# Involution stage: the running maximum is taken chunk by chunk from PSUM, and ScalarE copies the weights of GpSimd's taps

## The chip, the cores and the metric

The kernel runs on one core of one Trainium2 chip. The metric is the device time of one execution in microseconds. Five engines run side by side and meet at semaphores: TensorE (PE), VectorE (DVE), ScalarE (ACT), GpSimd (POOL) and SyncE (SP, which only issues DMAs here).

## The reference, cut to what matters

The program is an involution layer followed by attention and a token-routed feed-forward layer. Only the involution is touched. Per pixel it computes 49 weights (a 7x7 window) for each of 32 channel groups, takes a softmax over the 49, and sums 49 shifted copies of the projected image with them:

```
sub2 = x1[:, :, None] - unfold_patches(x2)
y = relu(bn_eval(feat, ...))            # 34 channels x 49 taps x pixels
y = conv1x1(y, cw1)
y = relu(bn_eval(y, ...))
wgt = softmax(conv1x1(y, cw2, cb2), axis=2)     # over the 49 taps
for i in range(K):
    for j in range(K):
        out = out + patch(i, j) * wgt[:, :, idx][:, :, None]
```

The softmax subtracts the maximum over the taps, and its denominator is summed beside the products (as a ninth plane) and divided out at the end.

## The kernel before

The 56x56 image is cut into 14 blocks of 4 rows; 128 partitions hold 4 images x 32 groups. `conv_stage` works on two blocks at once in a slot: for the next block `a` it makes the logits (the chain), for the current block `b` it forms and sums the 49 products. There are 15 slots: the first has only `a`, the last only `b`, and 13 have both. `slots` writes them out for each engine, the middle ones inside a loop. Every engine runs its own list in program order.

In a slot the steps u = 0 to 19 are "pairs": DVE multiplies the weights of two taps with the window (`pair`, 39 taps) into one of two `prod` buffers; the last 10 taps are GpSimd's `own` products. PE adds every tap's nine planes to the accumulators in PSUM banks 4 to 7 through an identity matrix (`add`). ACT copies the weights of a pair twice: to PSUM banks 2 and 3 for DVE (`weights`) and into the ninth plane of `prod` for PE (`denominators`).

The chain of block `a` goes through 14 chunks c (half a kernel row each), one for each step u = c + 1 (`CH_AT`). A chunk passes PE `first` (two matmul groups), ACT `second` (ReLU from PSUM), PE `second`, ACT `third` (adds the bias and writes the logits `lg`). All chunks of a slot with both blocks use the same two PSUM banks, so PE's `first` of a chunk waits until ACT's `third` of the chunk before has emptied them. GpSimd's `z` and ACT's `first(i)` (a ReLU) prepare the input of each kernel row i. DVE takes the maximum of the logits row by row (`rowmax`, 6 instructions) and folds the 7 columns of a row (`fold`, 3 instructions) into `mx`; GpSimd subtracts it (`shift`), ACT exponentiates (`expo`). For block `a`, GpSimd does `shift` 0 and 1 at the end of the slot, behind `own(8)`; ACT follows with `expo` 0 and 1 and `weights` 0, after which the next slot's first pair can start.

GpSimd's `own` has two buffers, so `own(k)` waits until PE has added `own(k-2)` (`own_used`), which PE does at step u = 8 + k, behind that step's pair.

```
OWN_AT = [NPAIR_D - OWN + k for k in range(OWN)]      # 10 .. 19
POOL_ORDER = [..., ("own", 0), ("own", 1), ("z", 6)] + [("own", k) for k in range(2, OWN - 1)]
```

Of the kernel before, what the change touches and what calls it, by code (L numbers as in the profile page):

```python
# [339 lines left out]
NMAX = K7 + 1  # L340


class Blk:
# [24 lines left out]
def conv_stage(nc, planes, x2_dram, a1_dram, pf_dram, cw1_bd, cw2_bd, ident_dram, conv_dram, keep):  # L368
    ctx = ExitStack()
    with ctx:  # L370
# [73 lines left out]
        @block.gpsimd  # L444
        def _(pool):
            def z(a, i):
                q = a.q(i)
                if i == 0:
                    pool.wait_ge(x_in[a.par], 32 * (a.half + 1))
                if not (a.early(1) and i < 2):  # L450
                    pool.wait_ge(mm1, 2 * (q - 1))
                o = y1[a.qpar(i)][:].rearrange("p j (h w) -> p j h w", w=W)
                x1 = a1[a.par][:].rearrange("p (h w) -> p h w", w=W).unsqueeze(1).broadcast_to([P, K7, RW, W])
                row = x2w[a.par][:, i:i + RW, 0:W]
                x2 = bass.AP(row.tensor, row.offset, [row.ap[0], [1, K7], row.ap[1], row.ap[2]])
                pool.tensor_tensor(o, x1, x2, ALU.subtract).then_inc(z_ready, 1)  # L456

            def shift(b, i):
                pool.wait_ge(maxed, b.n + 1)
                if not b.early(1):  # L460
                    pool.wait_ge(den_in, NPAIR_D * (b.n - 1) + FREE_ROW_PAIRS if i < FREE_ROW else NPAIR_D * b.n)
                if i == FREE_ROW and not b.early(1):
                    pool.wait_ge(own_ready, 2 * OWN * b.n)
# [80 lines left out]
        def _(act):  # L544
# [18 lines left out]
            def denominators(b, p):  # L563
# [2 lines left out]
                    act.wait_ge(summed, NPAIR_D * b.n + p - 1)  # L566
                act.activation(prod[p % 2][:, 0:n, :, SHARE], tap_pair(p), ACT.Copy).then_inc(den_in, 1)

            def slot(a, b):
                def first(i):  # L570
                    act.wait_ge(z_ready, a.q(i) + 1)
# [14 lines left out]
                def third(c):  # L586
                    act.wait_ge(mm2, a.g(c) + 1)
                    i, h, k = c // 2, c % 2 * 2, chain_bank(b, c)
                    if b and c % 2 == 0:
                        act.wait_ge(shifted, b.q(i) + 1)  # L590
                    act.activation(lg[:, i, h:h + 2].rearrange("p h j w -> p h (j w)"), ps[:, k:k + 2, 0:CW],  # L591
                                   ACT.Identity, bias=par[:, CB2:CB2 + 1]).then_inc(logit, 1)

                if b is None:
                    first(0)
                    for c in range(NCH):
                        second(c)
                        if c >= 1:
                            third(c - 1)
                        if c % 2 == 0 and c + 2 < NCH:  # L600
                            first(c // 2 + 1)
                    third(NCH - 1)
# [30 lines left out]
        def _(v):  # L633
# [9 lines left out]
                                den.unsqueeze(2).broadcast_to([P, B, SHARE, W]), ALU.mult).then_inc(divided, 1)  # L643

            def slot(a, b):
                def rowmax(i):
                    if i == 0:
                        return
                    v.wait_ge(logit, a.g(2 * i + 2))
                    if i == 1 and b and not b.early(1):  # L650
                        v.wait_ge(divided, 2 * b.n)
                    if i > 1:
                        v.wait_ge(ranmax, NMAX * a.n + i - 1)
                    v.tensor_tensor(run[:], lg[:, i], lg[:, 0] if i == 1 else run[:], ALU.max).then_inc(ranmax, 1)

                def fold():
                    v.wait_ge(ranmax, NMAX * a.n + K7 - 1)
                    v.tensor_tensor(run[:, :, 0:3], run[:, :, 0:3], run[:, :, 4:7], ALU.max).then_inc(ranmax, 1)
                    v.wait_ge(ranmax, NMAX * a.n + K7)
                    v.tensor_tensor(run[:, :, 0:2], run[:, :, 0:2], run[:, :, 2:4], ALU.max).then_inc(ranmax, 1)  # L660
                    v.wait_ge(ranmax, NMAX * a.n + K7 + 1)
                    if b:
                        v.wait_ge(shifted, K7 * a.n)
                    v.tensor_tensor(mx[:].rearrange("p (h w) -> p h w", w=W), run[:, :, 0], run[:, :, 1], ALU.max).then_inc(maxed, 1)  # L664

                def pair(p):
                    n = min(2, ND - 2 * p)
# [27 lines left out]
        def _(pe):  # L695
# [5 lines left out]
            def slot(a, b):  # L701
                def first(c):
                    i, hh = c // 2, c % 2
                    if hh == 0:
                        pe.wait_ge(relu1, a.q(i) + 1)
                        pe.wait_ge(pf_in[a.qpar(i)], 16 * B * a.qhalf(i))
                    k = chain_bank(b, c)
                    if b is None:
                        if c >= 2:
                            await_ge(logit, a.g(c) - 1)  # L710
# [33 lines left out]

                def pair(p, k):
                    if k == 0:
                        pe.wait_ge(den_in, NPAIR_D * b.n + p + 1)
                        await_ge(prod_ready, NPAIR_D * b.n + p + 1)
                    mm = add(prod[p % 2][:, k], p == 0 and k == 0, False)
                    if 2 * p + k == min(2 * p + 1, ND - 1):  # L750
                        mm.then_inc(summed, 1)

                def own(k):
                    await_ge(own_ready, 2 * (OWN * b.n + k + 1))
                    mm = add(own_buf[k % 2], False, k == OWN - 1)
                    if k < OWN - 1:
                        mm.then_inc(own_used, 1)
# [1726 lines left out]
```

## Time and profile before

| what | value |
|---|---|
| time, median of 3 executions | 3697.45 us (3691.7 to 3697.88) |
| profiled execution, span from first to last instruction | 3768.7 us (no other time of this execution is on record) |
| PE busy | 3044.6 us (81%) |
| DVE busy | 2563.3 us (68%) |
| ACT busy | 2010.5 us (53%) |
| POOL busy | 2040.6 us (54%) |
| mean granted TensorE clock | 0.919 |

The span is 71.25 us longer than the median of the timed executions. The involution's slots lie between about 235 us and 1714 us of it; the shares above mix them with the rest. In the timeline rows quoted below, a number in square brackets is the engine's idle time just before, with what ended it.

### The profile page before, as it was taken

The numbers are of one execution on the slowest core, as the hardware profiler recorded it, in microseconds if no ns is written. First come the engines' busy times: TensorE is split into PE (matmuls) and PEld (weight loads), VectorE is DVE, ScalarE is ACT, GpSimd is POOL, SyncE is SP. The second block draws the span as 40 slices with busy tenths as digits, with TensorE's granted clock in tenths as the row PEclk, the third lists the DMA queues.
The fourth block names the chain that finished last, engine by engine and source line by source line (L and its number), as shares of the span: only waits on it lengthen the run. The fifth ranks groups of instructions, "written<-read, shape, count | busy, mean of one in ns | idle before, by whom it ended". The sixth has DMA issues, their size and how long they took to land. (4 is left out here: it accounts for less than half of the span.)

```text
span 3768.7 us, 102003 instructions
## 1 busy us (share of the span) xinstructions
PE 3044.6 (81%) x42638; PEld 1539.3 (41%) x42638; DVE 2563.3 (68%) x2229; ACT 2010.5 (53%) x3451; POOL 2040.6 (54%) x1112
## 2 busy tenths in 40 slices
PE   4767788877777788764999899989999987586797
PEld 1224444433443444432433434343435343364565
DVE  6359999999999999996745755574667456443212
ACT  1175566666555566632676666657566754333120
POOL 1169888889898888874622434060416123332422
PEclk9889999999899999896999999999999998797898
DMA  5621111211111112103111111210221112343344
GB/s 195 194 76 47 58 37 58 61 58 59 52 56 50 57 35 61 51 12 97 27 27 64 41 27 37 74 29 19 61 69 28 27 45 98 115 132 113 123 134 127
DMA packets 169418, 257.31 MB, mean 68 GB/s; under 512 B 81584, under 2 KB 128600, under 8 KB 165912
## 3 DMA queue, kind: packets, MB, share of 16 engines
q1 hardware_dynamic: 157120, 219.82, 19.2%
q0 software_dynamic: 11360, 30.95, 2.6%
q8 instruction: 357, 5.85, 0.6%
q14 instruction: 77, 0.63, 0.1%
q10 hardware_dynamic: 504, 0.05, 0.0%
HBM read 152.23 MB, written 79.27 MB: 61 GB/s over the span
## 5 line engine op out<-in xcount | busy, mean ns | idle before, releaser
L741 PE MATMUL ps<-prod,ident 32*32 32x504 f32 x17472 | 936.4, 646 | 259.4 <-issue 182.7
L678 DVE TENSOR_TENSOR prod<-ps,win 128x3584 f32<-128x3584 f32 x280 | 1054.6, 3789 | 97.6 <-PE ps L741 50.9
L1405 POOL TENSOR_TENSOR pool<-kv 128x768 f32<-128x768 f32 (+1 forms) x200 | 349.8, 1756 | 541.5 <-ACT kv L1539 494.4
L741 PEld LDWEIGHTS ps<-prod,ident 32*32 32x32 f32 x17472 | 382.7, 108 | 464.1 <-issue 412.5
L1583 ACT ACTIVATE phq<-ps 128x896 f32<-128x896 f32 x448 | 391.3, 919 | 80.4 <-PE ps L1915 76.8
L456 POOL TENSOR_TENSOR y<-a1w,x2w 128x1568 f32<-128x1568 f32 x98 | 346.0, 3538 | 132.0 <-PE ps L722 114.9
L465 POOL TENSOR_TENSOR ex<-lg,mx 128x1568 f32<-128x1568 f32 x98 | 345.1, 3541 | 16.1 <-DVE mx L664 15.9
L1915 PE MATMUL ps<-qst,sel 96*128 96x448 bf16 x1120 | 297.2, 362 | 17.0 <-ACT sx L1568 8.4
L560 ACT ACTIVATE ps<-ex 128x448 f32<-128x448 f32 x280 | 148.4, 533 | 296.6 <-DVE prod L678 296.6
L1690 DVE TENSOR_TENSOR pool<-ps,kv 128x1280 f32<-128x1280 f32 (+1 forms) x200 | 295.4, 1480 | 1.1 <-ACT ps L1543 1.1
L482 POOL TENSOR_TENSOR own_a<-ex,win 128x1792 f32<-128x1792 f32 x70 | 262.2, 3746 | 45.9 <-issue 21.6
L482 POOL TENSOR_TENSOR osb<-ex,win 128x1792 f32<-128x1792 f32 x70 | 266.9, 3813 | 32.4 <-PE ps L741 32.4
L584 ACT ACTIVATE y<-ps,u2c,s2c 128x784 f32<-128x784 f32 x189 | 189.1, 1000 | 165.0 <-PE ps L722 165.0
L1971 PE MATMUL ps<-phq,snt 128*32 128x448 f32 (+1 forms) x2240 | 272.6, 559 | 2.0 <-ACT phq L1585 2.0
L717 PE MATMUL ps<-y,cw1bd 32*32 32x392 f32 x3136 | 211.9, 508 | 51.9 <-DMA cwp<-cw1p 25.7
L1893 PE MATMUL ps<-pool,kv 128*32 128x288 f32 (+3 forms) x3200 | 236.8, 412 | 17.1 <-ACT pool L1548 10.3
L1872 PE MATMUL ps<-wkv_s,xt 128*128 128x256 f32 (+1 forms) x800 | 227.4, 409 | 21.3 <-ACT kv L1544 16.4
L2318 PE MATMUL ps<-xct,w_s 128*128 128x392 f32 x512 | 194.0, 526 | 57.9 <-ACT hid L2201 30.4
L591 ACT ACTIVATE lg<-ps,par 128x784 f32<-128x784 f32 x196 | 179.0, 913 | 82.8 <-PE ps L733 82.8
L1789 DVE TENSOR_TENSOR at<-ps,rd 128x448 f32<-128x448 f32 x56 | 35.0, 624 | 272.5 <-PE ps L1971 272.5
L1915 PEld LDWEIGHTS ps<-qst,sel 96*128 96x128 bf16 x1120 | 85.2, 99 | 322.2 <-ACT phq L1583 158.7
L733 PE MATMUL ps<-y,cw2bd 32*32 32x392 f32 x3024 | 193.4, 523 | 24.9 <-ACT y L584 21.8
(266 smaller groups left out, 5306.3 us busy)
## 6 DMA issues: line engine op xcount, KB each, us to landing
win<-planes SPq DMA_DIRECT2D x14, 2480.0 KB, 9.0
pf<-pf_dram SPq DMA_DIRECT2D x392, 55.1 KB
qst<-qsp SPq DMA_DIRECT2D x96, 196.0 KB, 4.8
planes<-stage SPq DMA_DIRECT2D x7, 1984.0 KB, 7.0
xs<-in_x SPq DMA_DIRECT2D x8, 1568.0 KB, 22.0
conv_dram<-osb SPq DMA_DIRECT2D x56, 224.0 KB, 4.9
t<-in_x SPq DMA_DIRECT2D x28, 448.0 KB, 4.0
xt<-conv_dram SPq DMA_DIRECT2D x28, 448.0 KB, 7.6
```

What stands on the lines that cost most here:

```text
L456: pool.tensor_tensor(o, x1, x2, ALU.subtract).then_inc(z_ready, 1)
L465: pool.tensor_tensor(ex[:, i], lg[:, i], m, ALU.subtract).then_inc(shifted, 1)
L482: pool.tensor_tensor(o[:, :, 0:SHARE], w.unsqueeze(2).broadcast_to([P, RW, SHARE, W]), xw, ALU.mult).then_inc(own_ready, 1)
L678: v.tensor_tensor(o, w, xw, ALU.mult).then_inc(prod_ready, 1)
L741: mm = pe.matmul(ps[32 * h:32 * h + 32, 4 + r, 0:DENC], diag(ident, r), x[32 * r:32 * r + 32, h].rearrange("p s w -> p (s w)"), start=begi ...
L1405: pool.tensor_tensor(phk[j % 2][0:r, :, ROT_V * DH:FLIN].rearrange("p h (r i) -> p h r i", i=DH), ki.unsqueeze(2).broadcast_to([r, HPG, RO ...
L1583: act.activation(dst, src, ACT.Square).then_inc(phq_done, 1)
L1690: v.tensor_tensor(phk[j % 2][0:r, :, DH:ROT_V * DH].rearrange("p h (r i) -> p h r i", i=DH), same.unsqueeze(2).broadcast_to([r, HPG, ROT_V ...
L1872: mm = pe.matmul(ps[0:r, 4 + j % 2, 0:HPG * DH + P], xn[:, k, j * P:j * P + r], wkv_s[:, k, hg, :], start=(k == 0), stop=(k == CH - 1))
L1893: pe.matmul(ps[DH * h:DH * h + DH, f, 0:hi - lo], kv[j % 3][0:r, v0:v0 + DH], phk[j % 2][0:r, h, lo:hi], start=(j == 0), stop=(j == NT - 1))
L1915: mm = pe.matmul(ps[:, h, 0:CT], sel[:, f, :], qst[:, h, ch(c)], start=True, stop=True)
L1971: mm = pe.matmul(ps[DH * h:DH * h + DH, out_bank(hg, c), 0:CT], snt[0:kr, f, DH * h:DH * h + DH], phq[k % 2][0:kr, h, :], start=(f == 0), ...
```

## The change

The maximum is no longer taken from `lg` by kernel row. From chunk 2 on, DVE reads each of the two PSUM banks of a chunk (392 elements), adds the bias and takes the maximum with what it has so far, in one instruction for each bank (`chunkmax`, 24 instructions in a slot), two steps behind the chunk's PE work. ACT's `third` is cut into two instructions, one for each bank, which change banks with DVE's two, and both stand one step later than before. The fold has 4 instructions, uses the freed PSUM banks, and stands ahead of pair 16 rather than of pair 17. PE's `first` now waits for DVE's two instructions as well, and stands behind the first tap of the step's pair. GpSimd's 10 copies of a slot are gone; ACT makes them (`own_denominators`) one step ahead of PE's use.

```diff
-MAX_AT = [CH_AT[2 * i + 1] + 3 for i in range(K7)]
+MAX_AT = [t + 2 for t in CH_AT]
 FOLD_AT = MAX_AT[-1]
-EXP_NOW = {FOLD_AT + 1: 0, FOLD_AT + 2: 1}
+EXP_NOW = {18: 0, 19: 1}
...
-                pool.tensor_copy(o[:, :, SHARE], w).then_inc(own_ready, 1)
...
+            def own_denominators(b, k):
+                t = ND + k
+                i, j = t // K7, t % K7
+                act.wait_ge(exped, b.q(i) + 1)
...
+                if k >= 2:
+                    act.wait_ge(own_used, (OWN - 1) * b.n + k - 1)
+                act.activation(own_buf[k % 2][:, :, SHARE], ex[:, i, :, j, :], ACT.Copy).then_inc(den_in, 1)
...
+                def third(c, q):
+                    i, h, k = c // 2, c % 2 * 2 + q, chain_bank(b, c) + q
+                    if q == 0:
+                        act.wait_ge(mm2, a.g(c) + 1)
...
+                    elif c >= 2:
+                        act.wait_ge(ranmax, NMAX * a.n + 2 * c - 3)
+                    act.activation(lg[:, i, h].rearrange("p j w -> p (j w)"), ps[:, k, 0:CW],
                                    ACT.Identity, bias=par[:, CB2:CB2 + 1]).then_inc(logit, 1)
...
-                    if a and u in CH_AT:
-                        second(CH_AT.index(u))
+                    if a and u - 1 in CH_AT:
+                        third(CH_AT.index(u - 1), 0)
                     if b and u + 2 < NPAIR_D:
                         weights(b, u + 2)
+                    if b and u + 1 in OWN_AT:
+                        own_denominators(b, OWN_AT.index(u + 1))
+                    if a and u - 1 in CH_AT:
+                        third(CH_AT.index(u - 1), 1)
                     if b and u + 1 < NPAIR_D:
                         denominators(b, u + 1)
                     if a and u in CH_AT:
-                        third(CH_AT.index(u))
+                        second(CH_AT.index(u))
...
+                def chunkmax(c):
+                    if c < 2:
+                        return
+                    for q in (1, 0):
+                        h, k = c % 2 * 2 + q, chain_bank(b, c) + q
+                        if q == 1:
+                            v.wait_ge(mm2, a.g(c) + 1)
...
+                        else:
+                            v.wait_ge(logit, 2 * a.g(c) + 1)
+                        so_far = (lg[:, 0, h] if c < 4 else run[:, h]).rearrange("p j w -> p (j w)")
+                        v.scalar_tensor_tensor(run[:, h].rearrange("p j w -> p (j w)"), ps[:, k, 0:CW], par[:, CB2:CB2 + 1], so_far,
+                                               ALU.add, ALU.max).then_inc(ranmax, 1)
...
+                    v.wait_ge(logit, 2 * a.g(NCH))
+                    v.tensor_tensor(three, rows[:, :, :, 0:3 * W], rows[:, :, :, 4 * W:], ALU.max).then_inc(ranmax, 1)
...
-                        await_ge(logit, a.g(c))
+                        if c >= 3:
+                            pe.wait_ge(ranmax, NMAX * a.n + 2 * c - 4)
+                        await_ge(logit, 2 * a.g(c))
...
-                    if a and u in CH_AT:
-                        first(CH_AT.index(u))
                     if b:
                         pair(u, 0)
                     if a and u in CH_AT:
+                        first(CH_AT.index(u))
+                    if b and 2 * u + 1 < ND:
+                        pair(u, 1)
+                    if a and u in CH_AT:
                         second(CH_AT.index(u))
```

On ACT, one step of a slot (here step u = 2) reads so before; L584 is `second`, L560 `weights`, L567 `denominators`, L591 `third`, L547 `expo`:

```order
L584 ACTIVATE y<-ps,u2c,s2c 128x784
L560 ACTIVATE ps<-ex 128x448
L567 ACTIVATE prod<-ex 128x8x56
L591 ACTIVATE lg<-ps,par 128x784
L547 ACTIVATE ex<-ex 128x1568
```

and so after (L608 is a half of `third`, L562 `weights`, L569 `denominators`, L598 `second`, L549 `expo`):

```order
L608 ACTIVATE lg<-ps,par 128x392
L562 ACTIVATE ps<-ex 128x448
L608 ACTIVATE lg<-ps,par 128x392
L569 ACTIVATE prod<-ex 128x8x56
L598 ACTIVATE y<-ps,u2c,s2c 128x784
L549 ACTIVATE ex<-ex 128x1568
```

The two halves of `third` now belong to the chunk before the one of `second` in the same step, and only `denominators` stands between them and `second`.

On PE, one step reads so before (L717 and L722 are `first`, L741 a tap's additions, L733 `second`):

```order
L717 MATMUL ps<-y,cw1bd 32x392 x8
L722 MATMUL ps<-pf,cwp 32x392 x8
L741 MATMUL ps<-prod,ident 32x504 x16
L733 MATMUL ps<-y,cw2bd 32x392 x8
L741 MATMUL ps<-prod,ident 32x504 x16
```

and so after, from the second tap of the step before on (L761 and L766 are `first`, L785 the additions, L777 `second`):

```order
L777 MATMUL ps<-y,cw2bd 32x392 x8
L785 MATMUL ps<-prod,ident 32x504 x16
L761 MATMUL ps<-y,cw1bd 32x392 x8
L766 MATMUL ps<-pf,cwp 32x392 x8
L785 MATMUL ps<-prod,ident 32x504 x16
```

`first` moved behind the pair's first tap, `second` behind its second.

On DVE, the end of a slot's list reads so before (L654 `rowmax`, L658 to L664 the fold, L678 pairs):

```order
L678 TENSOR_TENSOR prod<-ps,win 128x8x448 x2
L654 TENSOR_TENSOR run<-lg,run 128x1568
L658 TENSOR_TENSOR run<-run 128x4x168
L660 TENSOR_TENSOR run<-run 128x4x112
L664 TENSOR_TENSOR mx<-run 128x224
L678 TENSOR_TENSOR prod<-ps,win 128x8x448 x2
L678 TENSOR_TENSOR prod<-ps,win 128x4x448
```

and so after (L685 `chunkmax`, L694 to L702 the fold, L716 pairs):

```order
L716 TENSOR_TENSOR prod<-ps,win 128x8x448
L685 SCALAR_TENSOR_TENSOR run<-ps,par,run 128x392 x2
L694 TENSOR_TENSOR ps<-run 128x2x336
L696 TENSOR_TENSOR run<-ps,run 128x4x56
L698 TENSOR_TENSOR run<-ps,run 128x4x56
L702 TENSOR_TENSOR mx<-ps,run 128x224
L716 TENSOR_TENSOR prod<-ps,win 128x8x448 x3
L716 TENSOR_TENSOR prod<-ps,win 128x4x448
```

Pair 16 moved from ahead of the last maximum to behind the fold.

## Rows read from the trace of the kernel before

**Rows 1.** The page, part 1: busy time over the span.
```profile
span 3768.7 us, 102003 instructions
...
PE 3044.6 (81%) x42638; PEld 1539.3 (41%) x42638; DVE 2563.3 (68%) x2229; ACT 2010.5 (53%) x3451; POOL 2040.6 (54%) x1112
```

**Rows 2.** The instructions of line 664, one in each slot.
```profile
L664 DVE TENSOR_TENSOR mx<-run x14: 391/393/440, 235.3 to 1618.0; 128x224 f32<-128x224 f32 x14
```

**Rows 3.** One slot cut at three of ACT's `second`: busy time by engine.
```profile
core 0: us, PE busy (x) PEld busy (x) DVE busy (x) ACT busy (x) POOL busy (x), PEclk, DMA share, GB/s
1002.44:1042.88 40.44, 37.27 (x948) 16.74 (x942) 38.22 (x12) 37.42 (x46) 32.46 (x11) 1.00 0.20 48
1042.88:1067.99 25.11, 21.14 (x565) 13.08 (x549) 24.52 (x8) 14.30 (x19) 21.83 (x10) 0.93 0.13 38
1067.99:1108.26 40.27, 26.39 (x664) 13.60 (x652) 36.53 (x14) 13.07 (x20) 39.76 (x16) 0.83 0.19 71
```

**Rows 4.** ACT's timeline: start, duration, line; chunk 0 on, chunk 13, next slot.
```profile
1002.44 1.00 ACT L584 ACTIVATE y<-ps,u2c,s2c 128x784 f32<-128x784 f32 x1 [6.27 <-PE ps L722]
1003.35 0.54 ACT L560 ACTIVATE ps<-ex 128x448 f32<-128x448 f32 x1
1003.81 0.56 ACT L567 ACTIVATE prod<-ex 128x448 f32<-128x448 f32 x1
1004.58 0.91 ACT L591 ACTIVATE lg<-ps,par 128x784 f32<-128x784 f32 x1 [0.20 <-PE ps L733]
1005.39 1.50 ACT L573 ACTIVATE y<-y 128x1568 f32<-128x1568 f32 x1
1006.79 1.00 ACT L584 ACTIVATE y<-ps,u2c,s2c 128x784 f32<-128x784 f32 x1
...
1026.61 0.91 ACT L591 ACTIVATE lg<-ps,par 128x784 f32<-128x784 f32 x1 [0.20 <-PE ps L733]
...
1067.99 1.00 ACT L584 ACTIVATE y<-ps,u2c,s2c 128x784 f32<-128x784 f32 x1 [2.00 <-PE ps L722]
...
1108.26 1.00 ACT L584 ACTIVATE y<-ps,u2c,s2c 128x784 f32<-128x784 f32 x1 [5.57 <-PE ps L722]
```

**Rows 5.** PE's timeline: the `first` of a chunk.
```profile
1027.78 0.89 PE L717 MATMUL ps<-y,cw1bd 32*32 32x392 f32 x16 [0.16 <-issue]
1028.44 0.40 PE L722 MATMUL ps<-pf,cwp 18*32 18x392 bf16 x8
```

**Rows 6.** Groups by form (400 to 1700 us), then instructions of two lines (min/median/max).
```profile
L567 ACT ACTIVATE prod<-ex 128x224 f32<-128x224 f32 x12 | 4.7, 391 | 38.1 <-PE ps L741 38.1
...
L654 DVE TENSOR_TENSOR run<-lg,run 128x1568 f32<-128x1568 f32 x59 | 165.1, 2798 | 0.0
...
L658 DVE TENSOR_TENSOR run<-run x14: 857/907/909, 233.8 to 1613.0; 128x672 f32<-128x672 f32 x14
...
L660 DVE TENSOR_TENSOR run<-run x14: 624/3974/3989, 234.7 to 1613.9; 128x448 f32<-128x448 f32 x14
```

**Rows 7.** POOL's timeline at the end of a slot: `own(8)`, `shift` 0 and 1.
```profile
1082.76 3.89 POOL L482 TENSOR_TENSOR own_a<-ex,win 128x1792 f32<-128x1792 f32 x1
...
1086.92 7.04 POOL L465 TENSOR_TENSOR ex<-lg,mx 128x1568 f32<-128x1568 f32 x2
```

**Rows 8.** DVE's timeline: `mx`, the next slot's pair 0, its pairs 1 and 2.
```profile
1082.70 0.39 DVE L664 TENSOR_TENSOR mx<-run 128x224 f32<-128x224 f32 x1
...
1096.06 3.89 DVE L678 TENSOR_TENSOR prod<-ps,win 128x3584 f32<-128x3584 f32 x1 [2.91 <-ACT ps L560]
...
1103.48 7.84 DVE L678 TENSOR_TENSOR prod<-ps,win 128x3584 f32<-128x3584 f32 x2
```

**Rows 9.** PE while it adds pair 16, then pair 17 (windows); its `own(7)` (timeline).
```profile
1075.23:1077.54 2.31, 2.31 (x67) 0.83 (x64) 2.31 (x1) 0.98 (x2) 2.31 (x2) 1.00 0.04 7
1086.99:1091.02 4.03, 4.03 (x78) 1.82 (x92) 3.70 (x1) 0.79 (x2) 4.03 (x2) 0.50 0.01 4
...
1090.32 2.60 PE L741 MATMUL ps<-osb,ident 32*32 32x504 f32 x32
```

More of the change, by code:

```diff
@@ L339 @@
 SCALE_AT = 1
-NMAX = K7 + 1
+NDEN = NPAIR_D + OWN
+NMAX = 2 * (NCH - 2) + 3
 class Blk:
@@ L460, in shift @@
                 if not b.early(1):
-                    pool.wait_ge(den_in, NPAIR_D * (b.n - 1) + FREE_ROW_PAIRS if i < FREE_ROW else NPAIR_D * b.n)
+                    pool.wait_ge(den_in, NDEN * (b.n - 1) + FREE_ROW_PAIRS if i < FREE_ROW else NDEN * b.n)
                 if i == FREE_ROW and not b.early(1):
-                    pool.wait_ge(own_ready, 2 * OWN * b.n)
+                    pool.wait_ge(own_ready, OWN * b.n)
+                if i == K7 - 1:
+                    pool.wait_ge(logit, 2 * b.g(NCH))
                 m = mx[:].rearrange("p (h w) -> p h w", w=W).unsqueeze(2).broadcast_to([P, RW, K7, W])
@@ L567, in denominators @@
                 act.activation(prod[p % 2][:, 0:n, :, SHARE], tap_pair(p), ACT.Copy).then_inc(den_in, 1)
+            def own_denominators(b, k):
+                t = ND + k
+                i, j = t // K7, t % K7
+                act.wait_ge(exped, b.q(i) + 1)
+                if k == 0 and not b.early(1):
+                    act.wait_ge(acc_done, b.n)
+                if k == 1 and not b.early(1):
+                    act.wait_ge(stored, 16 * RW * b.n)
+                if k >= 2:
+                    act.wait_ge(own_used, (OWN - 1) * b.n + k - 1)
+                act.activation(own_buf[k % 2][:, :, SHARE], ex[:, i, :, j, :], ACT.Copy).then_inc(den_in, 1)
             def slot(a, b):
@@ L584, in second @@
                     act.activation(o, ps[:, k:k + 2, 0:CW], ACT.Relu, scale=s2c[:], bias=u2c[:]).then_inc(relu2, 1)
[L586 to L591, printed above, removed]
+                def third(c, q):
+                    i, h, k = c // 2, c % 2 * 2 + q, chain_bank(b, c) + q
+                    if q == 0:
+                        act.wait_ge(mm2, a.g(c) + 1)
+                        if b and c % 2 == 0:
+                            act.wait_ge(shifted, b.q(i) + 1)
+                    elif c >= 2:
+                        act.wait_ge(ranmax, NMAX * a.n + 2 * c - 3)
+                    act.activation(lg[:, i, h].rearrange("p j w -> p (j w)"), ps[:, k, 0:CW],
                                    ACT.Identity, bias=par[:, CB2:CB2 + 1]).then_inc(logit, 1)
@@ L598, in slot @@
                         if c >= 1:
-                            third(c - 1)
+                            third(c - 1, 0)
+                            third(c - 1, 1)
                         if c % 2 == 0 and c + 2 < NCH:
                             first(c // 2 + 1)
-                    third(NCH - 1)
+                    third(NCH - 1, 0)
+                    third(NCH - 1, 1)
                     expo(a, 0)
@@ L645, in slot @@
             def slot(a, b):
-                def rowmax(i):
-                    if i == 0:
+                def chunkmax(c):
+                    if c < 2:
                         return
[L649 to L654, printed above, removed]
@@ L656, in fold @@
-                def fold():
[L657 to L661, printed above, removed]
+                    for q in (1, 0):
+                        h, k = c % 2 * 2 + q, chain_bank(b, c) + q
+                        if q == 1:
+                            v.wait_ge(mm2, a.g(c) + 1)
+                            if c < 4:
+                                v.wait_ge(logit, 2 * a.g(c - 2) + 2)
+                            else:
+                                v.wait_ge(ranmax, NMAX * a.n + 2 * c - 6)
+                            if c == 2 and b and not b.early(1):
+                                v.wait_ge(divided, 2 * b.n)
+                        else:
+                            v.wait_ge(logit, 2 * a.g(c) + 1)
+                        so_far = (lg[:, 0, h] if c < 4 else run[:, h]).rearrange("p j w -> p (j w)")
+                        v.scalar_tensor_tensor(run[:, h].rearrange("p j w -> p (j w)"), ps[:, k, 0:CW], par[:, CB2:CB2 + 1], so_far,
+                                               ALU.add, ALU.max).then_inc(ranmax, 1)
@@ new lines, in fold @@
+                def fold():
+                    three = ps[:, 0:2, 0:RW // 2 * 3 * W].rearrange("p b (h x) -> p b h x", x=3 * W)
+                    rows = run[:].rearrange("p (b h) j w -> p b h (j w)", b=2)
+                    left = rows[:, :, :, 0:W]
+                    v.wait_ge(ranmax, NMAX * a.n + 2 * NCH - 4)
+                    v.wait_ge(logit, 2 * a.g(NCH))
+                    v.tensor_tensor(three, rows[:, :, :, 0:3 * W], rows[:, :, :, 4 * W:], ALU.max).then_inc(ranmax, 1)
+                    v.wait_ge(ranmax, NMAX * a.n + 2 * NCH - 3)
+                    v.tensor_tensor(left, three[:, :, :, 0:W], rows[:, :, :, 3 * W:4 * W], ALU.max).then_inc(ranmax, 1)
+                    v.wait_ge(ranmax, NMAX * a.n + 2 * NCH - 2)
+                    v.tensor_tensor(left, three[:, :, :, W:2 * W], left, ALU.max).then_inc(ranmax, 1)
+                    v.wait_ge(ranmax, NMAX * a.n + 2 * NCH - 1)
@@ L662, in fold @@
                     if b:
                         v.wait_ge(shifted, K7 * a.n)
-                    v.tensor_tensor(mx[:].rearrange("p (h w) -> p h w", w=W), run[:, :, 0], run[:, :, 1], ALU.max).then_inc(maxed, 1)
+                    v.tensor_tensor(mx[:].rearrange("p (b h w) -> p b h w", b=2, w=W), three[:, :, :, 2 * W:], left, ALU.max).then_inc(maxed, 1)
                 def pair(p):
@@ L681, in slot @@
                     if a and u in MAX_AT:
-                        rowmax(MAX_AT.index(u))
+                        chunkmax(MAX_AT.index(u))
                     if a and u == FOLD_AT:
@@ L707, in first @@
                     k = chain_bank(b, c)
+                    if c == 0 and not a.early(1):
+                        pe.wait_ge(maxed, a.n)
                     if b is None:
+                        if c >= 4:
+                            pe.wait_ge(ranmax, NMAX * a.n + 2 * c - 6)
                         if c >= 2:
-                            await_ge(logit, a.g(c) - 1)
+                            await_ge(logit, 2 * a.g(c) - 2)
                     else:
-                        await_ge(logit, a.g(c))
+                        if c >= 3:
+                            pe.wait_ge(ranmax, NMAX * a.n + 2 * c - 4)
+                        await_ge(logit, 2 * a.g(c))
                     y, f = y1[a.qpar(i)], pf[a.qpar(i)]
@@ L746, in pair @@
                     if k == 0:
-                        pe.wait_ge(den_in, NPAIR_D * b.n + p + 1)
+                        pe.wait_ge(den_in, NDEN * b.n + p + 1 + sum(t <= p for t in OWN_AT))
                         await_ge(prod_ready, NPAIR_D * b.n + p + 1)
@@ L753, in own @@
                 def own(k):
-                    await_ge(own_ready, 2 * (OWN * b.n + k + 1))
+                    pe.wait_ge(den_in, NDEN * b.n + OWN_AT[k] + k + 1)
+                    await_ge(own_ready, OWN * b.n + k + 1)
                     mm = add(own_buf[k % 2], False, k == OWN - 1)
```

2 lines of the change are left out of this document (removed).

## The prediction

> **What bounds the kernel now.** I looked first at where the involution lies and how often its pattern repeats. The line that writes `mx` runs once a slot, from 235.3 to 1618.0 us [rows 2]: 13 intervals of 106.4 us, 1383 us of the 3768.7 us span. DVE's 68% over the span [rows 1] is a mean over stages and says nothing here. So I cut one slot (1002.44 to 1108.26, 105.82 us) at three of ACT's `second` [rows 3]. DVE is busy 38.22 + 24.52 + 36.53 = 99.27 us of it, 94%; POOL 94.05, PE 84.80, ACT 64.79. By totals DVE bounds the slot, and the change takes work from DVE. But the stretches differ. In the first (chunks 0 to 9) ACT is busy 37.42 of 40.44 us. Its timeline shows why: `second`, `weights`, `denominators`, `third`, a ReLU or exponential, and the next `second` 4.35 us after the last, with one gap of 0.20 us [rows 4]. That order is a dovetail: the 1.50 us item hides PE's `first`, the two copies hide PE's `second`. In the last stretch POOL is busy 39.76 of 40.27 us: its serial tail (`own(8)`, two `shift`, then `expo` and `weights` on ACT) ends in a DVE wait of 2.91 us [rows 7, 8]. So DVE's work, the chain through ACT and PE, and POOL's tail lie within a few us of each other, and what counts is the circle: `second` of chunk 0 to that of chunk 13 takes 65.55 us (1002.44 to 1067.99), and from there to the next chunk 0 it takes 40.27 us [rows 4].
>
> **DVE's gain.** Six `rowmax` of 2.80 us = 16.8 us go [rows 6]. No row has an instruction of 392 elements that reads one operand from PSUM. With GpSimd idle, 448 elements took 0.62 us (the shortest of L660), 224 took 0.39 [rows 6, 2]; the line between gives 0.56 for 392, so 24 cost 13.4 us, and 0.48 by overlap would make 11.5. The fold drops from 0.91 + 3.97 + 0.39 = 5.3 us to 0.91 + 3 x 0.39 = 2.1. DVE saves 6.5 to 8.5 us a slot, if it bounds. POOL loses ten copies; ACT gets ten of 0.39 us [rows 6] and 14 more instructions.
>
> **The chain, after.** Within one ACT step it now runs: half `third`, `weights`, half `third`, `denominators`, `second`, ReLU/`expo`. PE's `first` of a chunk cannot begin until the second half of the previous chunk's `third` has ended, and ACT's `second` of that same chunk is two instructions later. So PE's `first`, hidden before, stands in the open behind one 0.5 us copy. Its price: `third` of 1026.61 ended at 1027.52, PE's `first` began at 1027.78 and its last matmul ended at 1028.84 [rows 4, 5]: 1.32 us from the end of `third` to a `second`. (Where PE is already running, 1.25 is possible.) A half `third` has no row either: a whole one of 784 takes 0.91, and ACT's copies of 448 and 224 take 0.56 and 0.39, or 0.76 us per 1000 elements [rows 4, 6], so 0.91 - 392 x 0.76/1000 = 0.61 for a half; the low bound, from the copies' own line at 392, is 0.50. I take 0.60, of which 0.09 overlaps its successor, as in rows 4. One step from `second` to `second`: 0.91 (`second`) + 1.40 (ReLU/`expo`) + 0.51 + 0.46 (`weights`) + 0.60 + 1.30 = 5.18 us, against 4.35.
>
> The Trainium skill (VectorE: DVE Perf Modes, on the trn2 errata) puts ScalarE at 172 cycles plus one per element from PSUM at 1.2 GHz. For 784 elements that is 0.80 us, and this trace has 0.91; for 392 it is 0.47. By it the chain's step would be 4.92 us rather than 5.18, and the chain would cost nothing in the sum below.
>
> Chunks 0 to 7 are 7 such steps, 36.3 us. From chunk 8 on an own copy of 0.30 stands ahead of the second half: 4 steps of 5.48 = 21.9 (the ReLU/`expo` items end at u = 11). The last two have no such item, and wait 2.14 us from `second` to `third` as in rows 4: 2.14 + 0.51 + 0.46 + 0.30 + 0.60 + 1.30 = 5.31 each, 10.6. Sum 68.8 us against 65.55: **+3.3 us a slot**. With halves of 0.50 and 1.25 for PE it is 13 x 0.25 less, +0.0; with 0.61 and 1.32, +3.8.
>
> **The tail, after**, counted from `second` of chunk 13 (before: `mx` at +14.7, `shift` at +18.9, pair 0 at +28.1, next chunk 0 at +40.27; rows 4, 7, 8). The halves of `third` end at 2.14 + 0.51 + 0.46 + 0.30 + 0.60 = 4.0. The fold takes 2.2 with its gaps, so `mx` comes at 6.3, eight us earlier than before. What follows does not profit in full: `shift` stands behind `own(8)` on POOL, `own(8)` waits for PE to add `own(6)` at step 16, and pair 16 now comes after the fold. Pair 16 ends at 6.3 + 3.9 = 10.2; PE adds it (2.3, rows 9) and `own(6)` (1.14), at 13.7; `own(8)` 3.7 and then, as before, 7.0 for two `shift` and 2.1 to pair 0 [rows 7, 8]: 26.6. That is the low bound.
>
> Two rows speak for more. The fold's first instruction reads two SBUF operands, as L660 does. L660 took 0.62 us in the first slot, where POOL is idle, and 3.97 in the middle one [rows 6]: it sat out a POOL product. L658, directly behind a `rowmax`, never did. After the change there is an instruction on PSUM ahead of it, and POOL's `own(6)` runs from about +3.1 to +6.8, so `mx` comes at 9.0. And PE then idles some 6 us before pair 16; behind such a pause it added pair 17 in 4.03 us instead of 2.31, at a granted clock of 0.50 (1.2 GHz) instead of 1.00 (2.4 GHz), and `own(7)` ended 5.9 us after that start [rows 9]. With both, pair 0 comes at 9.0 + 3.9 + 6.0 + 3.7 + 9.1 = 31.7.
>
> The skill (GPSIMD Engine Reference, section Specifications) says that GpSimd's SBUF interfaces are shared with VectorE instructions that have two SBUF inputs. By it the fold waits (+2.7) each time; by L658's row alone it would not.
>
> From pair 0 to `second` of chunk 0 it was 12.2 us. PE's `first(0)` now stands behind the first tap of pair 1, whose product ends at 1103.48 + 3.84 = 1107.32 [rows 8]; 0.1 + 1.15 for the tap + 1.1 for `first` gives 1109.7, 1.4 later than 1108.26. So the tail is 26.6 + 13.6 = 40.2 at least and 45.3 at most: -0.1 to +5.0 us. Nothing tells me how often the two delays meet; I take the middle, **+2.5**.
>
> **The sum.** 13 x (3.3 + 2.5) = 75.4 us. In the first slot 13 halves cost about 0.2 each and the fold saves 1.5: +1. The last slot has no chain. The profiled span would grow from 3768.7 to about 3845; the same us on the timed median, 71.25 lower, give 3697.45 + 76.4 = 3773.9. The bounds: 13 x (0.0 - 0.1) = -1 to 13 x (3.8 + 5.0) + 1 = +115, or 3696 to 3813.
>
> **Rivals.** *DVE's relief wins (faster).* If the chain is not what DVE waits for, a slot falls from 105.82 by 6.5 to 8.5, 85 to 110 us in all: 3587 to 3613. For it: DVE is busy 94% of the slot, and the steps around chunks 10 to 13 (25.11 us for 4) are DVE's today. Against it: a DVE step with both maxima is 3.84 + 2 x 0.48 = 4.8 us, and ACT's step is 5.18. It decides at one place, the open stretch between the second half of `third` and `second`: if `first` took 0.8 us there instead of 1.3 and the halves 0.50, the step would be 4.5, DVE would bound it, and the chain would end 5 us or more earlier a slot.
> *Break-even.* Halves of 0.50 and no delay in the fold: the low bounds meet, 3696 +- 7.
> *Both tail delays every slot, halves of 0.61:* 3813; part of my case's range.
> *The copies don't leave POOL's path:* ACT's own copy waits for PE's `own(k-2)` and holds the second half of `third` behind it. PE ends that addition about 0.8 us into the step, the copy's turn is at 0.97; with the slow clock there it slips by 0.5 a step for five steps, 13 x 2.5 = +33 us more, 3806.
>
> **How the numbers follow.** A difference of 0.2% (7 us) is what a measurement of this kernel can tell from none. Chain-bound and slower, 3705 to 3830: 0.69. Break-even: 0.10. DVE's relief, in full or in part (3587 to 3690): 0.21. The range from 3675 to 3825 leaves out most of the faster case (0.16) and the top of mine (0.03); my case's own range is 3715 to 3820.
>
> **What the profile after would show.** (1) ACT idle 0.7 to 0.9 us ahead of `second` in each step, put down to PE's `first`, and `second` to `second` near 5.2 us in chunks 0 to 7. (2) A `third` half near 0.60 us, `chunkmax` 0.48 to 0.56. (3) DVE busy about 91 to 93 us of a slot of 109 to 114, with waits for PE or ACT in every step. (4) `mx` 6 to 9 us after chunk 13's `second`, yet pair 0 at 26.6 to 31.7. (5) L694 at 0.9 us or, where it waits for POOL, 2 to 4. It would be wrong if ACT's gap ahead of `second` were absent, or if the interval between two `mx` were below 106 us.

## The result

The changed kernel takes 3778.85 us (median of 4, 3774.75 to 3780.62) against 3695.51 us (4 runs): a ratio of 1.0223, 95% interval 1.0210 to 1.0236. It is slower by 83.3 us where 76.4 were forecast; the time itself lies 5 us above the forecast 3773.9. Nearly all of it arises in the involution: the last multiplication of the divide starts at 1716.0 us in the profile before and at 1798.4 in the one after, 82.4 us later. The profiled span of before, 3768.7 us, hides this beside 3776.5: from that multiplication to its end it takes 2052.7 us, the one after 1978.1. The last experiment shows that this goes with the chip.

The page of the changed kernel, part 1; it answers to [rows 1]:

```profile
span 3776.5 us, 103754 instructions
...
PE 3041.0 (81%) x42638; PEld 1468.9 (39%) x42638; DVE 2535.6 (67%) x2495; ACT 2077.9 (55%) x3787; POOL 1902.7 (50%) x972
```

DVE lost only 28 us and POOL 138, while ACT gained 67. Now the same circle as in [rows 3], cut at `second` of chunk 0, chunk 9, chunk 13 (windows, columns as there); the third row is the tail before it:

```profile
1052.89:1099.21 46.32, 37.76 (x951) 14.80 (x939) 41.78 (x24) 39.27 (x57) 30.98 (x10) 1.00 0.17 42
1099.21:1120.49 21.28, 20.64 (x560) 10.03 (x550) 20.10 (x13) 15.85 (x26) 16.43 (x5) 1.00 0.16 46
1006.77:1052.89 46.12, 28.25 (x667) 13.78 (x655) 35.44 (x16) 14.48 (x24) 37.23 (x11) 0.74 0.17 64
```

Chunks 0 to 9 take 46.3 us against 40.4. There the order of ACT was a dovetail and is one no more. Chunks 9 to 13 take 21.3 against 25.1: here DVE's relief is real. The tail takes 46.1 against 40.3, at a mean granted clock of 0.74 against 0.83.

One step on ACT (timeline), which answers to [rows 4]:

```profile
1055.19 0.58 ACT L608 ACTIVATE lg<-ps,par 128x392 f32<-128x392 f32 x1
1055.66 0.55 ACT L562 ACTIVATE ps<-ex 128x448 f32<-128x448 f32 x1
1056.13 0.58 ACT L608 ACTIVATE lg<-ps,par 128x392 f32<-128x392 f32 x1
1056.60 0.58 ACT L569 ACTIVATE prod<-ex 128x448 f32<-128x448 f32 x1
1057.96 1.00 ACT L598 ACTIVATE y<-ps,u2c,s2c 128x784 f32<-128x784 f32 x1 [0.78 <-PE ps L766]
1058.87 1.50 ACT L549 ACTIVATE ex<-ex 128x1568 f32<-128x1568 f32 x1
```

The second half of `third` ends at 1056.71 and `second` starts 1.25 us later. One copy lies between, and 0.78 us of idle time are put down to PE's `first` (L766). The next `second` is at 1063.03: a step of 5.07 us. With an own copy it is 5.35, without a ReLU or exponential 5.29.

The tail, on DVE, PE and POOL (timelines), which answers to [rows 7 to 9]; chunk 13's `second` was at 1006.77:

```profile
1010.84 3.58 DVE L694 TENSOR_TENSOR ps<-run 128x672 f32<-128x672 f32 x1 [0.70 <-ACT lg L608]
...
1015.40 0.39 DVE L702 TENSOR_TENSOR mx<-ps,run 128x224 f32<-128x224 f32 x1
1015.71 7.68 DVE L716 TENSOR_TENSOR prod<-ps,win 128x3584 f32<-128x3584 f32 x2
...
1038.06 3.89 DVE L716 TENSOR_TENSOR prod<-ps,win 128x3584 f32<-128x3584 f32 x1 [8.37 <-ACT ps L562]
```

```profile
1019.74 4.02 PE L785 MATMUL ps<-prod,ident 32*32 32x504 f32 x64 [6.52 <-DVE prod L716]
1023.07 2.02 PE L785 MATMUL ps<-own_a,ident 32*32 32x504 f32 x32
```

```profile
1009.99 3.71 POOL L485 TENSOR_TENSOR own_a<-ex,win 128x1792 f32<-128x1792 f32 x1 [1.59 <-PE ps L785]
1013.64 4.32 POOL L485 TENSOR_TENSOR osb<-ex,win 128x1792 f32<-128x1792 f32 x1
1025.26 3.74 POOL L485 TENSOR_TENSOR own_a<-ex,win 128x1792 f32<-128x1792 f32 x1 [7.30 <-PE ps L785]
1028.96 6.99 POOL L468 TENSOR_TENSOR ex<-lg,mx 128x1568 f32<-128x1568 f32 x2
```

Read it in order of time. The fold's wide instruction (L694) is issued while POOL works on `own(6)` and ends 0.7 us after it. `mx` comes at +8.6 us rather than +14.7, and nobody can use it: POOL stands idle for 7.30 us in front of `own(8)`, until PE has added pair 16 and `own(6)`. PE had idled 6.52 us and does this slowly. The shifts begin 13.2 us after `mx`, and DVE waits 8.37 us at pair 0, where it waited 2.91.

Over all slots, from the starts of `second` of chunks 0 and 13 in ACT's timeline (chain: mean of 13; tail: mean of 12):

| kernel | chain, us | tail, us | sum |
|---|---|---|---|
| before | 65.84 | 41.07 | 106.91 |
| changed | 67.90 | 45.27 | 113.17 |
| e4, fold behind pair 16 | 67.94 | 40.67 | 108.61 |
| e10, other order on ACT | 64.49 | 45.38 | 109.87 |
| e8, both | 64.29 | 40.39 | 104.68 |

### The profile page after: what moved, and what is told of

Read it like the earlier page. It is cut to its first block and busy times, and to the rows that moved or that the text cites. A ratio compares the mean times of both kernels' runs of the same rounds, so it can differ in the third digit from the quotient of the medians.

```text
span 3776.5 us, 103754 instructions
## 1 busy us (share of the span) xinstructions
PE 3041.0 (81%) x42638; PEld 1468.9 (39%) x42638; DVE 2535.6 (67%) x2495; ACT 2077.9 (55%) x3787; POOL 1902.7 (50%) x972
## 5 line engine op out<-in xcount | busy, mean ns | idle before, releaser
L716 DVE TENSOR_TENSOR prod<-ps,win 128x3584 f32<-128x3584 f32 x280 | 1056.5, 3789 | 139.7 <-ACT ps L562 116.8
L785 PE MATMUL ps<-prod,ident 32*32 32x504 f32 x17472 | 856.2, 638 | 194.4 <-DVE prod L716 116.2
L785 PEld LDWEIGHTS ps<-prod,ident 32*32 32x32 f32 x17472 | 345.7, 107 | 446.9 <-issue 396.7
L457 POOL TENSOR_TENSOR y<-a1w,x2w 128x1568 f32<-128x1568 f32 x98 | 319.5, 3267 | 231.0 <-PE ps L766 212.8
L562 ACT ACTIVATE ps<-ex 128x448 f32<-128x448 f32 x280 | 148.6, 534 | 287.4 <-DVE prod L716 287.4
L598 ACT ACTIVATE y<-ps,u2c,s2c 128x784 f32<-128x784 f32 x189 | 189.7, 1004 | 170.4 <-PE ps L766 170.4
L761 PE MATMUL ps<-y,cw1bd 32*32 32x392 f32 x3136 | 181.7, 501 | 121.1 <-ACT lg L608 76.2
L608 ACT ACTIVATE lg<-ps,par 128x392 f32<-128x392 f32 x392 | 225.8, 580 | 45.7 <-PE ps L777 45.3
L685 DVE SCALAR_TENSOR_TENSOR run<-ps,par,run 128x392 f32<-128x392 f32 x280 | 171.4, 625 | 50.9 <-PE ps L777 43.0
L785 PE MATMUL ps<-osb,ident 32*32 32x504 f32 x2240 | 125.9, 673 | 93.2 <-POOL osb L485 85.1
```

Of the source, the lines that this page charges most:

```text
L716: v.tensor_tensor(o, w, xw, ALU.mult).then_inc(prod_ready, 1)
L785: mm = pe.matmul(ps[32 * h:32 * h + 32, 4 + r, 0:DENC], diag(ident, r), x[32 * r:32 * r + 32, h].rearrange("p s w -> p (s w)"), start=begi ...
```

## The experiments

Ratios are to runs of the kernel before on the same chip. Chips differ: on one, both kernels that ran there took about 75 us more behind the involution, so ratios are compared across chips, and microseconds within one chip or per slot.

**e1: the copies alone.** The ten own copies go from GpSimd to ScalarE, in the kernel before:

```diff
-                pool.tensor_copy(o[:, :, SHARE], w).then_inc(own_ready, 1)
...
                         weights(b, u + 2)
+                    if b and u + 1 in OWN_AT:
+                        own_denominators(b, OWN_AT.index(u + 1))
```

> The kernel before, with only the ten own copies of a slot moved from GpSimd to ScalarE (between weights and denominators); maximum, fold and the order on PE as before. Theory (the loss is the open stretch of the chain and the tail): neither is touched, and GpSimd's serial tail loses the copies behind own(6), own(7) and own(8) (1.9, 0.8 and 0.4 us in one slot), so that the two shifts begin as soon as mx is there and DVE's wait of 2.9 us ahead of pair 0 goes: about -2.5 us a slot, 3655 to 3680 us, ratio 0.990 to 0.995. Rival (ScalarE's copies, which wait for PE's addition, hold the chain): 3700 to 3740, slower than before.

Measured: 3728.18 us, ratio 1.0078 (1.0061 to 1.0095), slower. My theory failed. The rival was right about the wait and wrong about the place: the chain does not grow (65.34 us a slot for 65.84), the tail does (43.86 for 41.07). The group of the first fold instruction (min/median/max) and one slot's DVE, POOL and ACT timelines show where it went; chunk 13's `second` was at 1083.27, L579 is `own_denominators`:

```profile
L672 DVE TENSOR_TENSOR run<-run x14: 859/4212/4229, 232.8 to 1639.0; 128x672 f32<-128x672 f32 x14
```

```profile
1092.95 4.20 DVE L672 TENSOR_TENSOR run<-run 128x672 f32<-128x672 f32 x1
1097.19 4.00 DVE L674 TENSOR_TENSOR run<-run 128x448 f32<-128x448 f32 x1
...
1091.23 5.20 POOL L483 TENSOR_TENSOR osb<-ex,win 128x1792 f32<-128x1792 f32 x1
1096.39 4.31 POOL L483 TENSOR_TENSOR own_a<-ex,win 128x1792 f32<-128x1792 f32 x1
1101.87 6.99 POOL L466 TENSOR_TENSOR ex<-lg,mx 128x1568 f32<-128x1568 f32 x2 [1.16 <-DVE mx L678]
...
1110.51 0.39 ACT L579 ACTIVATE osb<-ex 128x224 f32<-128x224 f32 x1 [3.83 <-PE ps L755]
1110.81 0.37 ACT L567 ACTIVATE prod<-ex 128x224 f32<-128x224 f32 x1
1111.09 2.90 ACT L547 ACTIVATE ex<-ex 128x1568 f32<-128x1568 f32 x2
```

Before, that instruction took 0.91 us at the median [rows 6]; here 4.21. It ends with one POOL product, and the next wide one (L674) with the next. In the kernel before a POOL copy stood between two products (1075.91 to 1077.85 in the slot of [rows 8], held up by DVE's last `rowmax`). L658 started at 1077.66, when that copy was ending, and took 0.91 us; the product behind the copy took 4.26 us instead of 3.71. So what POOL's copies gave DVE was a turn between two products; that reading rests on the traces. The kernel before (timelines):

```profile
1077.66 0.91 DVE L658 TENSOR_TENSOR run<-run 128x672 f32<-128x672 f32 x1
...
1075.91 1.94 POOL L483 COPY own_a<-ex 128x224 f32<-128x224 f32 x1
1077.82 4.26 POOL L482 TENSOR_TENSOR osb<-ex,win 128x1792 f32<-128x1792 f32 x1
```

With the copies gone `mx` comes 3.3 us later. But this does not make the shifts late: they begin at +18.6 us, where they began at +18.9. The late fold pushes pair 17 back, PE adds `own(7)` behind pair 17, and ACT's last own copy waits 3.83 us for that. Both `expo` stand behind it in ACT's list, so pair 0 comes at +31.3 instead of +28.1. Before, only the last `denominators` stood there, which waits for pair 17 alone, and the second `expo` still waited 1.15 us for its `shift`. The move brought a wait into ACT's list, ahead of the two items that the next slot needs first.

**e2: the copies back on GpSimd,** in the changed kernel:

```diff
+                pool.tensor_copy(o[:, :, SHARE], w).then_inc(own_ready, 1)
...
-                    if b and u + 1 in OWN_AT:
-                        own_denominators(b, OWN_AT.index(u + 1))
```

> The changed kernel, with the ten copies back on GpSimd; everything else as changed. Theory (open stretch and tail): the chain loses six copies of 0.28 us (-1.7 us a slot), the tail gains one GpSimd copy of 0.4 to 1.9 us; 3755 to 3780 us, still 1.6 to 2.3% slower than before. Rival (the copies on ScalarE are the loss): near 3700.

Measured: 3772.59 us, ratio 1.0200 (1.0183 to 1.0217). This is inside the expected range. The move of the copies is not the loss; it lies in the rest of the change. Per slot the chain falls by 1.7 us, as expected (66.20 for 67.90), and the tail grows by 1.1 (46.39 for 45.27).

**e3: nothing in the open stretch.**

```diff
+                    if b and u + 1 < NPAIR_D:
+                        denominators(b, u + 1)
                     if a and u - 1 in CH_AT:
                         third(CH_AT.index(u - 1), 1)
-                    if b and u + 1 < NPAIR_D:
-                        denominators(b, u + 1)
```

> The changed kernel, with ScalarE's denominators of a step ahead of the second half of third instead of behind it: the same instructions, but nothing stands any more between that half and second. Theory (PE's first lies in the open there): the gap ahead of second grows from 0.78 to about 1.25 us and a step from 5.07 to about 5.5; 0.47 us x 13 steps x 13 slots = +79, 3840 to 3865 us. Rival (DVE or the sum of ScalarE's work sets the step): no change, 3775 to 3785.

Measured: 3862.74 us, ratio 1.0447 (1.0429 to 1.0464): by the ratios some 83 us more than the changed kernel, from the order of two instructions. ACT's timeline has the gap as forecast, and the next `second` is 5.53 us later:

```profile
1005.38 0.58 ACT L608 ACTIVATE lg<-ps,par 128x392 f32<-128x392 f32 x1
1007.21 1.00 ACT L598 ACTIVATE y<-ps,u2c,s2c 128x784 f32<-128x784 f32 x1 [1.25 <-PE ps L766]
```

A step that DVE or the sum of ACT's work had set would not have moved.

**e4: the fold behind pair 16.**

```diff
-FOLD_AT = MAX_AT[-1]
+FOLD_AT = MAX_AT[-1] + 1
```

> The changed kernel with FOLD_AT one higher: the fold behind pair 16 rather than ahead of it. Theory (the tail runs from pair 16 over PE's addition of own(6) to own(8) and the shifts): pair 16 ends some 5.5 us earlier, PE adds own(6) without a pause before it, and although mx comes about 4 us later, the shifts begin 6 to 8 us earlier; 13 x 7 = -90 us, 3675 to 3710 us. Rival (mx sets the tail): shifts and pair 0 come 4 us later, +50, 3820 to 3840 us.

Measured: 3716.07 us, ratio 1.0048 (1.0032 to 1.0065): 1.75 points off the changed kernel's 1.0223, and 6 us above the expected range. One slot on DVE, PE, POOL and ACT (timelines):

```profile
1091.14 4.23 DVE L694 TENSOR_TENSOR ps<-run 128x672 f32<-128x672 f32 x1
1096.35 0.39 DVE L702 TENSOR_TENSOR mx<-ps,run 128x224 f32<-128x224 f32 x1
...
1091.37 2.35 PE L785 MATMUL ps<-prod,ident 32*32 32x504 f32 x56 [1.05 <-DVE prod L716]
...
1094.98 3.93 POOL L485 TENSOR_TENSOR own_a<-ex,win 128x1792 f32<-128x1792 f32 x1 [0.34 <-PE ps L785]
1098.88 7.00 POOL L468 TENSOR_TENSOR ex<-lg,mx 128x1568 f32<-128x1568 f32 x2
...
1106.25 0.39 ACT L581 ACTIVATE osb<-ex 128x224 f32<-128x224 f32 x1 [4.30 <-PE ps L785]
```

Chunk 13's `second` was at 1084.04, so `mx` comes 3.7 us later than in the changed kernel (+12.3 for +8.6) and the shifts 7.4 us earlier (+14.8 for +22.2). PE meets pair 16 after an idle 1.05 us and adds it in 2.35. The shifts still begin behind `own(8)`, not behind `mx`. Pair 0 gains less than they do (+26.2 for +31.3, 5.1 us), because both `expo` now wait behind ACT's last own copy (L581, idle 4.30 us until PE has added `own(7)`), as in e1. The tail falls from 45.27 to 40.67 us and the chain stays (67.94).

**e5: the shifts ahead of `own(8)`,** in the changed kernel:

```diff
-... + [("own", k) for k in range(2, OWN - 1)]
+... + [("own", k) for k in range(2, OWN - 2)]
                 if a:
                     shift(a, 0)
                     shift(a, 1)
                 if b:
+                    own(b, OWN - 2)
                     own(b, OWN - 1)
```

> The changed kernel with own(8) moved behind the two shifts on GpSimd's list; fold still ahead of pair 16. Theory (the shifts are late because they stand behind own(8), which waits for PE's addition of own(6)): the shifts begin once own(7) is done, some 10 us earlier; ScalarE's exponentials then wait for its own copies of step 18, so pair 0 comes about 6 us earlier a slot: 3695 to 3715 us. Rival (DVE's pairs or the divide behind own(9) set the slot's end): at most 2 us a slot, 3750 to 3780.

Measured: 3708.34 us, ratio 1.0024 (1.0013 to 1.0035). The other way around the same wait: early fold, but the shifts no longer stand behind `own(8)`. They begin at +11.1 us, the tail takes 39.81 and the chain stays (67.70). So it is that place in the queue, and not the fold's position as such, that cost the tail.

**e7: the copies on ScalarE and the new fold, nothing else.** e1 with the four-instruction fold through PSUM, for which PE's `first` of chunk 0 also waits for `mx`, as in the changed kernel:

> The kernel before with the own copies on ScalarE (as in e1) and, besides, the changed kernel's fold of four instructions, of which only the first reads two SBUF operands; the maximum by rows, the chain and PE's order as before. Theory (e1 lost because both wide fold instructions wait for a GpSimd product, now that GpSimd's products follow each other without a copy): one of the two waits of about 3.3 us goes, mx comes 3 to 4 us earlier and the shifts follow own(8): 3 us a slot less than e1, 3680 to 3695 us. Rival (the copies hurt through ScalarE or PE): as e1, 3720 to 3735.

Measured: 3691.28 us, ratio 0.9976 (0.9963 to 0.9988), faster than before. The first wide instruction still takes 4.22 us, the other three 0.39 each, and the second wait is gone. `mx` comes 3.2 us earlier than in e1, the shifts only 1.2 (+17.4), and pair 0 by 3.3 (+27.9): it follows pair 17 and ACT's last copy (idle 3.68 us), not the shifts. These parts of the change gain as they stand, without a repair.

**e8: both repairs.** e4, and ACT's two halves directly behind each other:

```diff
+                    if a and u - 1 in CH_AT:
+                        third(CH_AT.index(u - 1), 1)
                     if b and u + 2 < NPAIR_D:
                         weights(b, u + 2)
                     if b and u + 1 in OWN_AT:
                         own_denominators(b, OWN_AT.index(u + 1))
-                    if a and u - 1 in CH_AT:
-                        third(CH_AT.index(u - 1), 1)
```

> e4 (fold behind pair 16) with the two halves of third directly behind each other, and weights and the own copy behind them, so that three items rather than one stand between the second half and second. Theory (PE's first in the open is what stretched the chain): steps without maxima fall from 5.07 to about 4.7, steps with an own copy from 5.35 to about 5.07, where DVE (3.8 + 1.25 us) binds: 2.6 us a slot, 3675 to 3690 us. Rival (DVE binds all steps, or weights come too late for DVE): 3710 to 3740.

Measured: 3671.47 us, ratio 0.9921 (0.9904 to 0.9937), faster than both kernels, and 3.5 us below the expected range. ACT's and DVE's timelines:

```profile
1002.73 1.05 ACT L608 ACTIVATE lg<-ps,par 128x392 f32<-128x392 f32 x2
1003.66 0.56 ACT L562 ACTIVATE ps<-ex 128x448 f32<-128x448 f32 x1
1005.03 1.00 ACT L598 ACTIVATE y<-ps,u2c,s2c 128x784 f32<-128x784 f32 x1 [0.32 <-PE ps L766]
...
1012.28 1.17 DVE L685 SCALAR_TENSOR_TENSOR run<-ps,par,lg 128x392 f32<-128x392 f32 x2
1013.37 3.88 DVE L716 TENSOR_TENSOR prod<-ps,win 128x3584 f32<-128x3584 f32 x1
1017.17 1.17 DVE L685 SCALAR_TENSOR_TENSOR run<-ps,par,run 128x392 f32<-128x392 f32 x2
```

The gap falls from 0.78 to 0.32 us and steps without maxima from 5.07 to 4.61. With maxima they are 4.89, and there DVE has no idle time left (1012.28 to 1017.17). So DVE does bind once the open stretch is filled, at 4.89 us. In the changed kernel both stood close together.

**e9: e8 with the shifts first.**

> e8 with own(8) behind the two shifts as well. Theory: the shifts begin with mx, 2 us earlier, but own(8) and own(9) then end later and the divide waits for them: 0 to 1.5 us a slot less than e8, 3660 to 3690 us. Rival (the divide is late): 3690 to 3720.

Measured: 3670.07 us, ratio 0.9919 (0.9903 to 0.9934). Not to be told from e8, though the shifts do begin 2 us earlier (+12.85 for +14.84). One slot on POOL and ACT (timelines), chunk 13's `second` at 1056.52:

```profile
1069.37 7.00 POOL L468 TENSOR_TENSOR ex<-lg,mx 128x1568 f32<-128x1568 f32 x2 [2.25 <-DVE mx L703]
...
1078.58 0.39 ACT L582 ACTIVATE osb<-ex 128x224 f32<-128x224 f32 x1 [4.16 <-PE ps L786]
...
1079.16 2.90 ACT L550 ACTIVATE ex<-ex 128x1568 f32<-128x1568 f32 x2
```

The `expo` of the first shift waits for the last own copy, and that for PE's `own(7)` behind pair 17; pair 0 comes at +26.1, in e8 at +26.2. What would be left to take in the tail is that copy's place ahead of `expo`. No run moved it.

**e10: the order of e8 alone,** in the changed kernel.

> The changed kernel with only ScalarE's order of e8 (both halves of third, then weights and the own copy); the fold stays ahead of pair 16. Theory (chain and tail are two separate losses that add): what the order gave on top of e4 (3716 to 3671 us, -45) it gives here too, 3725 to 3745 us. Rival (the tail of the changed kernel hides a shorter chain): 3765 to 3780.

Measured: 3810.30 us, ratio 1.0097 (1.0080 to 1.0114), on the chip on which the kernel before takes 3773.86. Off the changed kernel's 1.0223 that is 1.26 points, some 47 us, and e8 gave 1.27 on top of e4. The table above says the same per slot: the order moves only the chain, the fold only the tail, and the two add.

**e0: the kernel before again.**

> The kernel before once more, for a second profile. Its first profile spans 3768.7 us, 71 more than its timed runs, and matmuls of a later stage wait 57.9 us in it where the changed kernel's wait 6.0. If that is chance of one execution, this profile spans about 3695 us, with the involution's slots at 106.9 us as in the first. Rival (the profile stretches this kernel): 3760 to 3775.

Measured: 3769.74 us, a span of 3767.6. The rival's number came, but not its reason: on this chip the timed runs of the kernel before take 3773.86 us too. Its involution is as in the first profile (the last divide at 1718.3 us against 1716.0), and the feed-forward matmuls wait as there (groups of the second profile of before, then of the changed kernel's):

```profile
L2318 PE MATMUL ps<-xct,w_s 128*128 128x392 f32 x512 | 197.1, 533 | 53.0 <-issue 36.7 <-ACT hid L2201 14.8 <-ACT xct L2196 1.5
```

```profile
L2363 PE MATMUL ps<-xct,w_s 128*128 128x392 f32 x512 | 185.0, 509 | 6.0 <-ACT hid L2246 4.5 <-ACT xct L2241 1.5
```

From that divide to the end the first profile takes 2052.7 us, this one 2049.3 and e10's, on the same chip, 2054.2; the other nine take 1974 to 1984. So it goes with the chip. That the first profile came from this chip is not on record; it is what these numbers suggest. Why that chip's stage is slower was not looked into.

## Why the prediction was right

**The open stretch: right, shown by e3, e8 and e10.** Forecast steps of 5.18, 5.48 and 5.31 us; measured 5.07, 5.35 and 5.29. The gap ahead of `second` is 0.78 us, inside the 0.7 to 0.9 forecast. A half `third` takes 0.58 for my 0.60, and from its end to `second` it is 1.25 for my 1.30. The chain grew by 2.06 us a slot (67.90 - 65.84) where I had +3.3: the mechanism was right, the step's terms were each a little large, and the slot that I read (65.55) lies 0.3 below the mean. Two numbers of the low bound had no good source: 1.25 us for PE had no row behind it, and came out by luck; the copies' own line gives 0.52 for a half, not 0.50. e3 added 0.47 us to the stretch and the kernel grew by 83 us (0.47 x 13 x 13 = 79); e8 and e10 took 0.46 away and the time fell.

**The tail: right in mechanism, shown by e4 and e5, with a size mis-set.** I had bounds of -0.1 and +5.0 us and took the middle, +2.5. Measured is +4.20 (45.27 - 41.07), near the upper bound; in itself 45.27 is the upper bound's 45.3, since the slot that I read (40.27) lies 0.8 below the mean. L694 took 3.58 us at the median of its 14, and in the slot quoted pair 16 was added at a granted clock of 0.50 after PE's pause. In the slot quoted, `mx` came at +8.6 (bounds 6.3 and 9.0) and pair 0 at +31.3 (26.6 and 31.7). The term to correct is the choice of the middle: the rows had both delays, and nothing in them said that they would be rare. The first slot cost 3.5 us (its successor's chunk 0 at 258.11 for 254.58) where I had 1. The two errors, -1.2 and +1.7, nearly cancel: 5.8 forecast and 6.3 measured a slot. So the mechanisms are confirmed, but that the sum came so close is in part luck.

**DVE's relief: the term was too large.** I had 6.5 to 8.5 us a slot. DVE is busy 97.3 us of the quoted slot where it was 99.3. A maximum of 392 elements takes 0.626 us (I had 0.56), so 24 take 15.0, and the fold takes 4.8 rather than 2.1: by these numbers DVE saves 2.3 us. Two signs of my own list missed with it, `chunkmax` at 0.48 to 0.56 us and DVE busy 91 to 93 us of a slot. This rival could not have come about at the size that I gave it. What it stood on, that DVE binds once the chain is short, e8 shows at 4.89 us a step.

**The copies.** Alone they cost 0.78% (e1). In the changed kernel the difference of 0.2% is not shown by the times (1.0210 to 1.0236 against e2's 1.0183 to 1.0217); a slot of the traces is 0.6 us longer. I had costed them at 0.30 us each on ACT, and left out what they did on POOL's side and that the last one stands ahead of `expo`. Their rival, that ACT's wait for `own_used` holds the chain, did not come: before chunk 13's `second` no own copy of e1 shows a wait, and one of the changed kernel's does (1.66 us). In the tail that wait is real: 2.3 us in the changed kernel, where `expo` then waits 3.51 us more for POOL and so loses nothing by it, and 3.6 to 5.3 us in the slots of e1, e4, e7, e8 and e9, where it sets `expo`.

By which of the two delays the tail grows more was not separated by a run. In the slot quoted, L694's wait is 2.7 us (3.58 for 0.91), and from the start of pair 16's addition to the end of `own(6)`'s it is 5.35 us, where I had 3.4 without a pause. e4 keeps the first (L694 takes 4.23 us) and takes the second out of the shifts' path.

## What to carry to other kernels

Before moving an instruction in a list that runs in order, write down for each engine-to-engine latency which items cover it: here the same work in another order moved the kernel by some 83 us one way and 47 the other. A result that is ready earlier is worth nothing while its consumer stands in a queue behind something that the same edit made later; follow the queue to its last wait. An instruction that moves to another engine takes its wait along: look at what stands behind it in the new list. And an instruction that looks like overhead on one engine may be the gap in which another one gets its turn.

## What the runs showed of the hardware

- A DVE instruction with two SBUF operands does not share with a running GpSimd product, it waits for the end of it: 0.91 became 4.21 us in e1, 0.62 became 3.97 before, and `rowmax` (1568 elements) took 1.77 us at the least and 2.58 at the median. The POOL instruction waits likewise: a copy of 0.38 us took up to 1.96. Instructions with one operand in PSUM (the pairs, 3.88 us at the median and 3.89 at most; the maxima, 0.629 at most) do not stretch. The Trainium skill (GPSIMD Engine Reference, section Specifications) says that VectorE instructions with two SBUF inputs contend with GpSimd; the traces agree, and give the price as the rest of the other engine's instruction.
- The maximum of 392 elements from PSUM with a bias takes 0.615 to 0.629 us on DVE. The Trainium skill (VectorE: DVE Perf Modes, on the trn2 errata) would make it 120 cycles and one per element at 0.96 GHz, 0.53 us; the measurement decides. ACT's half of 392 took 0.58 us where that table gives 0.47.
- After 6.52 us of idle PE time the granted clock was 0.50 (1.2 GHz), and the 64 matmuls of a pair took 4.02 us, where a pair took 2.31 at 1.00 (2.4 GHz).
